# A two-layer graph network on one core: another front and passage, and the first layer's bias added by VectorE tile by tile instead of by TensorE

## What is computed

```python
h = max(layernorm(x), 0)
# layer one ("layer 0" in the code): linear part, and a mean over the neighbours
out   = h @ W_self.T + b_self
neigh = h[dst] @ W_neigh.T + b_neigh
agg   = segment_sum(neigh, src);  count = segment_sum(1, src)
x = x + out + agg / max(count, 1)
h = max(layernorm(x), 0)
# layer two ("layer 1" in the code): symmetric normalisation, no weights
norm = deg**-0.5 [src] * deg**-0.5 [dst]
x = x + relu(segment_sum(h[src] * norm, dst))
```

## Time and profile before

| | us |
|---|---|
| median of 3 runs (1183.37 to 1186.17) | 1185.05 |
| the profiled execution, its time | 1182.12 |
| its span, from the first instruction to the last | 1180.3 |

### The profile page before, as it was taken

How to read it: one execution, slowest core, us unless ns; L and a number is a source line. 1 busy time by engine, 2 the same in 40 slices (tenths; PEclk the granted TensorE clock), 3 DMA queues, 4 the chain that set the end, 5 groups by cost and what they waited for, 6 DMA issues and landing times.

```text
span 1180.3 us, 30320 instructions
## 1 busy us (share of the span) xinstructions
PE 1057.1 (90%) x9408; PEld 955.5 (81%) x9408; DVE 1057.1 (90%) x3040; ACT 1082.5 (92%) x2871; POOL 862.4 (73%) x1143
## 2 busy tenths in 40 slices
PE   1388999999999999999999993799999999999998
PEld 1377999999989988989889992688888888888886
DVE  7779989989989989989989853899999999999995
ACT  2378999999989999999999991999999999999997
POOL 4767777777777877777777714888888888888870
PEclk9689999999999999999999997555555555555555
DMA  6325666767666766776667526499999999999994
GB/s 209 120 71 166 209 197 207 222 190 215 190 202 200 197 214 188 208 198 204 208 194 216 186 98 235 133 297 293 291 282 288 288 282 292 281 285 289 288 288 168
DMA packets 82232, 259.39 MB, mean 220 GB/s; under 512 B 19987, under 2 KB 20357, under 8 KB 82117
## 3 DMA queue, kind: packets, MB, share of 16 engines
q1 hardware_dynamic: 58948, 210.86, 57.3%
q0 software_dynamic: 22400, 46.91, 13.7%
q10 hardware_dynamic: 768, 0.20, 0.1%
HBM read 152.93 MB, written 104.37 MB: 218 GB/s over the span
## 4 chain that ended last, share of the span: by engine, by line
ACT 56%; POOL 15%; issue 11%; DVE 7%; PE 7%; DMA 3%; POOLq 0%; ACTq 0%; DVEq 0%
ACT work L739 24%; ACT p_O L739 14%; POOL X L634 12%; ACT p_T L739 6%; ACT area L754 4%; ACT p_c L739 3%; ACT area L749 2%; DMA X<-in_x,IDX 2%; DVE ST L1333 2%; PE p_O L910 2%; ACT sd L717 2%; POOL work L596 1%; PE p_O L922 1%; POOL work L592 1%; DVE p_O L1376 1%
## 5 line engine op out<-in xcount | busy, mean ns | idle before, releaser
L739 ACT ACTIVATE work<-X,shift,scale 128x128 f32<-128x128 f32 x1372 | 564.7, 512 | 1.8 <-DVE shift L1367 1.8
L634 POOL DMA_INDIRECT X<-in_x,IDX x392 | 387.4, 988 | 127.4 <-issue 98.6
L1333 DVE BATCH_NORM_STATS2 ST<-X 128x6 f32<-128x256 f32 x1176 | 408.2, 415 | 26.7 <-DMA X<-in_x,IDX 24.9
L968 PE MATMUL p_O<-work 32*128 32x128 f32 x1984 | 307.0, 436 | 44.4 <-DVE work L1350 24.8
L634 POOL DMA_INDIRECT X<-x_table,IDX x294 | 286.3, 974 | 76.5 <-issue 61.7
L968 PEld LDWEIGHTS p_O<-work 32*128 32x128 f32 x1984 | 263.9, 323 | 87.8 <-ACT work L739 31.1
L910 PE MATMUL p_O<-wnT,area 128*128 128x128 f32 x1568 | 218.0, 283 | 0.0
L922 PEld LDWEIGHTS p_O<-wsT,area 128*128 128x128 f32 x1568 | 207.2, 193 | 7.6
L922 PE MATMUL p_O<-wsT,area 128*128 128x128 f32 x1568 | 207.8, 276 | 0.0
L739 ACT ACTIVATE p_O<-X,shift,scale 128x128 f32<-128x128 f32 x496 | 199.1, 442 | 0.6 <-DVE shift L1367 0.6
L910 PEld LDWEIGHTS p_O<-wnT,area 128*128 128x128 f32 x1568 | 193.0, 194 | 0.3 <-DVE area L1386 0.3
(11 more groups left out here) (173 smaller groups left out, 1191.9 us busy)
## 6 DMA issues: line engine op xcount, KB each, us to landing
x_table<-area SPq DMA_DIRECT2D x98, 528.0 KB
X<-x_table SPq DMA_DIRECT2D x98, 528.0 KB
X<-in_x SPq DMA_DIRECT2D x98, 512.0 KB, 4.6
out_x<-area SPq DMA_DIRECT2D x98, 512.0 KB, 6.9
X<-in_x,IDX POOLq DMA_INDIRECT x392
X<-x_table,IDX POOLq DMA_INDIRECT x294
moved<-held SPq DMA_DIRECT2D x32, 12.2 KB
es<-in_src SPq DMA_DIRECT2D x1, 488.5 KB, 3.5
```

The source lines that it names most:

```text
L634: nc.gpsimd.indirect_dma_start(got(s)[:, k, 0:w], None, table, bass.IndirectOffsetOnAxis(ap=IDX[:, s, k:k + 1], axis=0)).then_inc(gathered ...
L739: last = nc.scalar.activation(o, row(l, s, r), ACT.Relu, bias=shift[:, s, r:r + 1], scale=scale[:, s, r:r + 1])
L968: last = nc.tensor.matmul(outs1[p][g][:, P * col:P * col + P], SEL[1][q, p, part_of, :], H[1][q, p, draw, :], start=False, stop=(half == 1 ...
L1333: last = V.bn_stats(ST[:, s, r:r + 2, :].rearrange("p r k -> p (r k)"), pair.rearrange("p r c -> p c r"))
```

## The change

1. `scaled`: instead of one multiplication of 128x512 there are four instructions of 128x128 (scalar_tensor_tensor), which scale a tile by its count and add the bias, held for all partitions in `bias_all`. `selves` loses its bias matmul. `bias_all` is made once, by one small matmul at the end of the front and a copy by ACT; the three parts of the bias are made by POOL and ACT in turns, not by DVE.
2. Front: the loads of blocks 0 to 5 wait until the first window has landed; cutting and comparing the links comes behind the decoding of group 0; group 1's links are taken in later (`marks(1)` behind the statistics of block 0, `decode(1)` in step 6 instead of 3). `LOT[0]` becomes 2. For blocks 0 to 7 (`FIRST`) ACT normalises the last row too, and POOL's `last_row` returns at once. `START_AHEAD` and `STARTING` change the first 15 blocks. Slots 6 to 9 are loaded one after the other, as statistics get done.
3. The later groups begin at steps 7, 20, 33, 46, 59 instead of 3, 17, 31, 45, 58.
4. Passage: `dis2` is transposed in steps 82 to 85 inside `aggregate` and copied out there by ACT (`take_dis`), moved in steps 86 to 89 by DMAs on SP's queue, and added by DVE in step 93. SP issues the first loads of layer 1 behind the last stores of layer 0, from block 90 on.

```diff
-LOT = (5, 4)
+LOT = (2, 4)
-START_AHEAD = (1, 1, 1, 1, 2, 2, 2, 3, 3, 3)
+START_AHEAD = (1,) * 4 + (2,) * 5 + (3,) * 6
+STARTING = 7
+FIRST = 8
-    BEGIN = {2: 3, 3: 17, 4: 31, 5: 45, 6: 58}
+    BEGIN = {2: 7, 3: 20, 4: 33, 5: 46, 6: 59}
+    TURN_AT, PASS_AT, DIS_AT = 82, 86, 93
+    def rows_of(i):
+        return range(0, ROWS if i < FIRST else ROWS - 1)
-        return 1 if k == 2 else next((g for g in BEGIN if BEGIN[g] + 11 == k), None)
+        return 1 if k == 5 else next((g for g in BEGIN if BEGIN[g] + 11 == k), None)
+    def dis_groups(k):
+        return [g for g in range(TB) if TURN_AT + g // 2 == k]
...
 @block.sync
+                early = old + RING[0] - NB
+                if l == 0 and 0 <= early and old % RING[0] < RING[1]:
+                    b = old % RING[0]
+                    sp.wait_ge(stored[0][b % HR[0]], 16 * (b // HR[0] + 1))
+                    load(1, 0, b)
+            sp.wait_ge(s_win[0], 16)
             for s in range(EARLY):
                 load(0, 0, s)
...
             for s in range(EARLY, RING[0]):
+                sp.wait_ge(st_ready[0], s - EARLY + 2)
                 load(0, 0, s)
...
+                if k == PASS_AT:
+                    sp.wait_ge(s_disl, TB // 2 + 1)
+                    if PASS_AT + n // 4 == k:
+                        sp.dma_start(moved[to, 2, slot_of(of), :], DISL[of, j, :]).then_inc(s_moved, 16)
             def fast():
-                for s in range(RING[1]):
-                    load(1, 0, s)
...
 @block.gpsimd
+            pool.wait_ge(s_w, 64)
+            nc.gpsimd.tensor_tensor(bsum[0:1, 0, :], brow[0:1, 0, :], brow[0:1, 1, :], ALU.add).then_inc(s_bsum, 1)
+            for k in range(2):
+                pool.wait_ge(s_bpart, k + 1)
+                nc.gpsimd.tensor_tensor(bsum[0:1, (k + 1) % 2, :], bsum[0:1, k % 2, :], bpart[0:1, k, 0, :], ALU.subtract
+                                        ).then_inc(s_bsum, 1)
...
             def last_row(turn, off):
+                if i < FIRST:
+                    return
...
 @block.scalar
+            def take_dis(k):
+                act.wait_ge(s_disT, dis_groups(k)[-1] // 2 + 1)
+                for g in dis_groups(k):
+                    c = slice(GROUP_BLOCKS * g, GROUP_BLOCKS * g + GROUP_BLOCKS)
+                    for a in range(2):
+                        q = slice(SLOTS * a, SLOTS * a + SLOTS)
+                        last = nc.scalar.copy(DISL[q, :, c]..., turned_dis(g)[q, :]...)
+                last.then_inc(s_disl, 1)
             nc.scalar.copy(wnT[:, :], p_O[2][:, D:2 * D]).then_inc(s_wcopied, 1)
-            digit(0)
-            digit(1)
+            for k in range(3):
+                act.wait_ge(s_bsum, k + 1)
+                nc.scalar.copy(bpart[0:1, k, :, :], bsum[0:1, k % 2, :]...).then_inc(s_bpart, 1)
             take_codes(0)
-            for n in range(2, 2 * len(CUTS)):
+            for n in range(2 * len(CUTS)):
                 digit(n)
+            act.wait_ge(s_wT, 3)
+            nc.scalar.copy(bias_all[:, :], p_O[2][:, 2 * D:3 * D]).then_inc(s_wcopied, 1)
...
-                starting = off < len(START_AHEAD)
+                starting = off < STARTING
...
                 if joins_at(off) is not None:
                     take_codes(joins_at(off))
+                if dis_groups(off):
+                    take_dis(off)
...
-                    normalise(0, turn, off + 1, range(MID, ROWS - 1))
+                    normalise(0, turn, off + 1, rows_of(off + 1)[MID:])
...
             def fast():
-                act.wait_ge(s_disl, 1)
-                for to, of, j in moves():
-                    act.dma_start(moved[to, 2, slot_of(of), :], DISL[of, j, :]).then_inc(s_moved, 16)
...
 @block.tensor
             pe.wait_ge(s_bias, 48)
+            nc.tensor.matmul(p_O[2][:, 2 * D:3 * D], ones3[:, :], bias3[:, 0:D], start=True, stop=True).then_inc(s_wT, 1)
...
-                pe.wait_ge(row_ready, i + 1)
+                if i >= FIRST:
+                    pe.wait_ge(row_ready, i - FIRST + 1)
...
+                for g in dis_groups(off):
+                    pe.wait_ge(s_dis2, 1)
+                    last = nc.tensor.transpose(turned_dis(g), dis2[:, g, :, :]..., ident[0:TP, 0:TP])
+                if dis_groups(off):
+                    pe.wait_ge(s_disl, dis_groups(off)[-1] // 2 + 1)
...
                 pe.wait_ge(n_scaled[g], i + 1)
-                nc.tensor.matmul(out0(off, g)[:, :], ones3[:, :], bias3[:, :], start=False, stop=False,
-                                 skip_group_check=True)
...
-                if off == NB:
-                    pe.wait_ge(s_dis2, 1)
-                    ...
-                    for b in range(TB):
-                        turned_dis = nc.tensor.transpose(banks_dis[b // 4]..., dis2[:, b, :, :]..., ident[0:TP, 0:TP])
...
 @block.vector
-            dve.wait_ge(s_edges, 48)
-            cut_digit(0)
-            cut_digit(1)
             marks(0)
             code_links(0)
             for r in range(SLOTS // 8):
                 draw(0, r)
             double(0)
-            cut_digit(2)
+            dve.wait_ge(s_edges, 48)
+            cut_digit(0)
             decode(0)
-            for n in range(3, 2 * len(CUTS)):
+            for n in range(1, 2 * len(CUTS)):
                 cut_digit(n)
-            compare_edges()
+                if n < 4:
+                    compare_edges(n - 1)
-            split_bias()
...
                 bank = out0(off, g)[:, :].rearrange("p (a b) -> p a b", a=GT)
-                V.tensor_tensor(bank, bank, rc[:, off % 2, g:BT:2]...to_broadcast([P, GT, P]),
-                                ALU.mult).then_inc(n_scaled[g], 1)
+                for j in range(GT):
+                    last = V.scalar_tensor_tensor(bank[:, j, :], bank[:, j, :], rc[:, off % 2, 2 * j + g:2 * j + g + 1],
+                                                  bias_all[:, :], ALU.mult, ALU.add)
+                last.then_inc(n_scaled[g], 1)
```

More of the change, by code:

```diff
@@ L495, in general @@
             def general():
+                for s in range(RING[1]):
+                    sp.wait_ge(x_loaded[s], 16 * (len(range(s, NB, RING[0])) + 1))
                 sp.wait_ge(g_clean, 1)
@@ L876, in aggregate @@
                     turn_codes(joins)
+                for g in dis_groups(off):
+                    pe.wait_ge(s_dis2, 1)
+                    last = nc.tensor.transpose(turned_dis(g), dis2[:, g, :, :].rearrange("p a b -> p (a b)"), ident[0:TP, 0:TP])
+                    if g == dis_groups(off)[-1]:
+                        last.then_inc(s_disT, 1)
                 if off == SUM_AT:
@@ L975, in fast @@
             def fast():
-                pe.wait_ge(s_disl, 1)
-                nc.tensor.matmul(p_O[1][:, :], ones3[:, :], bias3[:, :], start=True, stop=True)
+                pe.wait_ge(sdeg_ready, NB)
                 nc.tensor.matmul(p_c[:, :], ones3[:, :], bias3[:, :], start=True, stop=True).then_inc(s_disT, 1)
@@ L1485, in then @@
                     dve.wait_ge(g_ord, order[0] if order[1] is None else order[1] + order[0])
+                for s in range(EARLY, RING[1]):
+                    dve.wait_ge(x_loaded[s], 16 * (len(range(s, NB, RING[0])) + 1))
                 dve.wait_ge(g_ord, 1)
```

98 lines of the change are left out of this document (42 added, 56 removed).

## The result

The changed kernel takes 1226.68 us (median of 4 runs, 1225.81 to 1230.38) where the kernel before, run beside it, took 1184.37: a ratio of 1.0364 (95% interval 1.0348 to 1.0381). It is 42 us slower; I had forecast 1178.7 and a range of 1166 to 1190. The profiled execution has a span of 1224.0 us against 1180.3, so 43.7 us are to be found.

The account below looks back on a forecast made before the run. POOL sets the pace at 6.60 us a block, ACT 0.2 below, DVE with 0.46 spare. 1182.1 - 8.3 (ramp) + 3.8 (blocks 12 to 97) - 1.8 (tail) = 1175.8 profiled, so 1178.7 against 1185.05; range 1166 to 1190.

Parts of the forecast that it names:

- The scaling: DVE in each block: four 128-column instructions at 0.20 us replace one of 0.58, twice, adding 0.45 us, to 6.59.
- (d): Rival: DVE becomes the limit above about 0.23 us an instruction; at 0.26, 20 us more, near 1198; chance 0.14.
- cover for the copies of `dis2`: Four ACT steps lengthened, 5.7 us together: free behind ACT's 0.2 a step of slack against POOL, otherwise 5.7.
- POOL's index copies: Layer 0, copies every second step: 0.07 us a block, 6 over blocks 12 to 97, mostly covered by POOL's 4 us lead.
- Blocks 12 to 97: Layer 0 after the start: 6.65 us a block for 6.60, 3.8 us later (4 earlier to 12 later).
- The front: Before block 0: window near 11, first gather 24.5, first root 38.7, block 0's aggregates copied near 48.8 instead of 57.95.
- The ramp: Blocks 0 to 12: block 7 at 104, steps 8 to 11 at 6.9, block 12 at 138.6, 8.3 us earlier.
- Tail and passage: End of layer 0 into layer 1: tail 1.8 us shorter, passage unchanged at 20.4 us, plus or minus 1.
- The early loads: Passage: layer 1's first loads may share engines with the last store, costing under 1 us, gaining as much.
- (e): Rival: TensorE's clock falls to 1.2 GHz from 2.4 for parts of layer 0; 1204 or more; chance 0.04.
- (b): Rival: the ramp's gain is kept, ACT sets the pace at 6.5 us a block; near 1167; chance 0.17.
- (c): Rival: the front gives little while blocks 12 to 97 lose the 3.8; 1182.7 to 1187.4; chance 0.17.

Follow-up runs that it names:

- o2: Kernel before with each 128x512 scaling cut into four plain tensor_tensor multiplies of 128x128, bias still on TensorE; ratio 1.0018.
- o3: Kernel before with each 128x512 scaling cut into two tensor_tensor multiplies of 128x256; ratio 1.002.
- q4: Kernel before with each scaling as four 128x128 tensor_scalar multiplies, per-partition factor, no third operand; ratio 1.0035.
- n3: Changed kernel with the old scaling and bias matmul put back and `STARTING` 12 instead of 7; 1185.06 us, ratio 1.0016.
- n1: Changed kernel with the old scaling: one 128x512 multiply on DVE, bias matmul back on TensorE; 1196.7 us, ratio 1.0101.
- n2: Changed kernel with `STARTING` 12 instead of 7, new scaling kept; 1215.75 us, ratio 1.0265.
- o1: Kernel before with the new scaling alone, `bias_all` made in the front; 1215.55 us, ratio 1.0258.
- p3: Changed kernel with old scaling, `STARTING` 12 and the turning of `dis2` back behind block 97; repeat of n5, ratio 1.0167.
- p4: Changed kernel with old scaling, `STARTING` 12, `dis2` turned behind block 97 and layer 1's first loads back behind layer 0's last stores; ratio 1.0172.
- q3: Kernel before with index copies for two blocks at a time instead of five (`LOT = (2, 4)`), third run; ratio 0.999.
- r2: Kernel before with the new scaling alone, repeated where the kernel before takes 1432 us; ratio 1.0029.
- q2: Repeat of p4: changed kernel with old scaling, `STARTING` 12, `dis2` turning and layer 1's first loads put back; ratio 1.0145.
- n5: Changed kernel with old scaling, `STARTING` 12 and the turning of `dis2` back behind block 97; ratio 1.0118.
- o4: Kernel before with index copies for two blocks at a time instead of five (`LOT = (2, 4)`), first run; ratio 0.9993.
- p2: Kernel before with index copies for two blocks at a time instead of five (`LOT = (2, 4)`), second run; ratio 1.001.

## Why the prediction was wrong

**What bounds the kernel.** The reading of the four engines held in part. DVE had 0.46 us a block to spare, and the change used up that and 0.4 more. But POOL doesn't set the pace alone: 53 of the 85 steps from block 12 to 97 of the kernel before take 6.39 to 6.42 us, ACT's own 6.40, and the chain there lies on ACT's normalising (24.5%) more than on POOL's gathers (20.4%). The mean of 6.60 comes from longer steps, up to 8.7 us, between them. I took a mean of the whole layer for the step of one engine, and so gave ACT a slack of 0.2 that most steps don't have.

**The scaling: the term that failed, by size.** Forecast +0.45 us a block on DVE, measured 1.00 - 0.59 = 0.41 for each of two scalings, +0.82. That takes DVE from 6.14 to 6.96; the window has 197.54 / 200 x 7.00 = 6.91 busy. I drew a line through the earlier trace rows and took its 0.20 for the new instruction. The line is right, for its own kind: o2 and o3 lie on it. But neither row has a per-partition scalar, and the form with it takes 0.05 to 0.06 us more each (q4), eight times a block. The point from which rival (d) decides was given as 0.23. Its own formula reaches the pace of 6.60 at 0.20 already (6.14 + 2 x (0.81 - 0.58) = 6.60); at 0.23 it gives 6.8. So the forecast had no margin at all on an unmeasured form, and a chance of 0.14 for (d) was too low. The Trainium skill's figure ("VectorE: DVE Perf Modes", The TRN2 errata), 120 cycles and the columns, gives 0.26, an estimate, and came nearest here. But as a rule it fails on the plain multiply of the same width, 0.20, and on the 512, 0.60 against 0.66. Why it agrees with this one form isn't shown.

**Where the 50 us are.** Against the forecast for the profiled execution, 1175.8, it took 1225.8. Block 12 came 17.3 us later than forecast, blocks 12 to 97 took 29.4 more, tail and passage 3.2 more.

**Blocks 12 to 97.** Forecast +3.8, measured +33.2. Of that the scaling makes 22 (594.6 - 572.8) to 28 (589.1 - 561.4). The rest, 11, is in n3. There my **cover for the copies of `dis2`** failed: I had them free behind POOL, or 5.7 us at most; they cost 4.5, because ACT's own 6.40 us set those steps, with nothing to wait for, and they took TensorE's matmuls into the wait. The other 6 to 7 us are not settled; I had 6 for POOL's index copies, most of it covered by POOL's lead, and the chain of n3 points there.

**The rival's price.** (d) had 20 us over the forecast, for 65 steps and on top of a gain of 8.3 in the ramp. Its 6.89 for an instruction of 0.26 doesn't follow from its formula, which gives 6.14 + 2 x (1.04 - 0.58) = 7.06, or 39 us over 6.60 in 85 steps: I had added 0.75, which takes a computed cost for the one of 512 where the trace has 0.58. Most of the 85 steps paid, and DVE's load reached the ramp as well: block 12 is 6.0 us earlier in n1 than in the kernel after, and 8.1 earlier in n3 than in n2.

**The front** was right. Window at 11.45 (near 11), first gather at 24.95 (24.5), bias copy 36.3 (37.3), table load behind it, first root 37.88 (38.7), block 0's copy 47.97 (48.8). The check matmuls are quicker, 4.23 us instead of 5.21.

**The ramp** had the right mechanism and a wrong size. Block 7 came at 109.9 (104), block 12 at 155.9 (138.6). I gave one wait for statistics of 3 us to step 7 and let steps 8 to 11 be "coupled" at 6.9. They took 9 to 11 each: a wait that goes round a ring of three engines came back in each of these steps. n3, with neither the new scaling nor the short start, has block 12 at 137.6; my 138.6 was the time of a ramp without either cost.

**Tail and passage.** Forecast -1.8, measured +1.4. Without the bias matmuls the tail does get shorter: from block 97's copy to the last addition it is 7.5 us instead of 9.0, and o1, which has only the scaling, needs 28.9 us from that copy to layer 1 instead of 29.4. But from the last addition to layer 1 it is 23.3 us, not the 20.4 of before and of the forecast. The early loads, for which I had "under 1 us", make 1.6 of these 2.9 (p3 against p4); the rest isn't taken apart.

**Rivals.** (d) happened. (e) did not: the granted clock is 1.00 with TensorE busy 87% of the stretch from 200 to 400. (b) and (c) are out. That DVE's 6.59 would have been free is not shown.

## What to carry to other kernels

Before moving work from one engine to another, price it by an instruction of the same form, operands and width in the trace: here the spare time was 0.46 us a block, the width of the eight instructions took 0.45 of it, and their form 0.4 more. TensorE, full but waited for by nobody, gave nothing back when it was relieved. Before naming the engine that sets the pace, look at single steps and not only at their mean. In a start where three engines wait for each other in turn, one wait put first in a step was paid in five steps of the ramp; test its length by itself, since it is one constant.

## What the runs showed of the hardware that I had not expected

**The per-partition scalar on VectorE.** Spacing of back-to-back instructions on PSUM: tensor_tensor 0.20 us at 128 columns, 0.335 at 256, 0.60 at 512; tensor_scalar and scalar_tensor_tensor with a per-partition factor 0.24 to 0.26 at 128 (the median of both is 0.258).

**The same instructions, another pace.** Where the kernel before takes 1432 to 1462 us, DVE's instructions have nearly the length they have at 1184 (in q3 and in the kernel before: statistics 415 ns in both, the multiply of 512 at 696 and 684), the clock is granted at 0.99 to 1.00 in layer 0 as well, and yet a block takes 7.7 to 7.9 us instead of 6.6. Layer 1 takes 578 to 602 us instead of 442.6, so more than half of the difference lies there, and I haven't taken it apart. In layer 0 each of ACT's steps waits once, for a releaser that the profile doesn't show, after TensorE's last count matmul, as in this stretch of r2 (TensorE's timeline, then ACT's):

```profile
407.41 0.17 PE L899 MATMUL p_c<-parts,ones 128*128 128x8 bf16 x1
```

```profile
409.74 1.07 ACT L757 COPY area<-p_T 128x512 f32<-128x512 f32 x2 [1.34 <-remote]
```

ACT's copy needs nothing but that matmul's signal, and comes 2.2 us after its recorded end; at 1184 it comes when ACT is free. The ends of matmuls are modelled in the profile, so a matmul that ended later than recorded would look the same. The front shows the same, larger, in q2 (TensorE, then ACT):

```profile
36.63 0.22 PE L904 MATMUL p_O<-bias,ones 128*128 128x128 bf16 x1
```

```profile
68.19 0.27 ACT L759 COPY bias_all<-p_O 128x128 f32<-128x128 f32 x1 [37.28 <-remote]
```

The copy of `bias_all` comes 31 us after the matmul, and the first root stands behind it. Block 0's aggregates are copied at 87.4 there, against 65.6 in q3, whose front is the old one. These 21.8 us are about what q2 loses against the kernel before (1456.7 - 1434.1 = 22.6). In n5, p3 and p4 block 0 comes some 20 us later than in o4 and p2, of the 19 to 27 us that they lose; so no verdict on the new front can be carried from one kind of chip to the other. That the copy stands ahead of the first root doesn't explain it by itself: r2 has the old front and the same copy there (TensorE, then ACT),

```profile
38.54 0.22 PE L857 MATMUL p_O<-bias,ones 128*128 128x128 bf16 x1 [1.32 <-DMA bias<-bpart]
```

```profile
55.80 0.27 ACT L714 COPY bias_all<-p_O 128x128 f32<-128x128 f32 x1 [26.15 <-remote]
```

and it comes 17 us late, yet block 0's aggregates are copied at 67.4. Why the delay is 31 us with the new front is open, and so is what delays TensorE's signals there at all: fewer matmuls didn't shorten the step (r2), and the records show none that is longer.
